# Router logits of a fused recurrence, linear and mixture-of-experts kernel: from eight float32 matmuls between the transposes to sixteen split-operand matmuls behind the first gate product

## The chip, the core and the metric

The kernel runs on one core of one Trainium2 chip. A core has TensorE (matmuls; in the profile PE, and PEld for the loads of its stationary operand), VectorE (DVE), ScalarE (ACT), GpSimd (POOL) and SyncE (SP), which here only issues transfers. Each engine goes through its own list of instructions in order, and they meet through semaphores. The metric is the device time of one execution in microseconds; lower is better.

## What is computed

The input x has 4 batches of 1024 tokens with 1024 channels. Two layers follow each other, and both first run a bidirectional recurrence over the sequence (exponential decay per channel), whose result multiplies the layer's input. The part that matters here stands behind the second recurrence. Cut to it, the reference says:

```
x = x + ffn0(cond(x, side))              # a 1024x1024 linear layer
c = cond1(x, side)                       # the second recurrence, gated
flat = rmsnorm(c, norm_w)                # z below
logits = flat @ router_w.T               # 32 experts
topk_w, topk_ids = top_k(softmax(logits), 4)
routed = sum over the 4 experts of topk_w * (silu(flat@w1_gate) * (flat@w1_up)) @ w2
shared = silu(flat @ sg) * (flat @ su) @ sd
out = x + routed + shared
```

All of it is float32. The large products are done on operands that were split in two parts in the type fp32r (a high part and the rest), as three matmuls: high by high, high by low, low by high. The router logits are a product of z (1024 channels) with 32 columns.

## The kernel before

Channels lie on the 128 partitions in `CB` = 8 blocks, and the 4096 tokens are worked through in `HALVES` = 8 halves of `HALF` = 512 tokens (`HT` = 4 tiles of 128). The program has three stages. In the first (to about 310 us) the recurrence runs alone, block by block ("units"), on DVE, ACT and POOL. In the second (to about 1990 us) TensorE computes the linear layer and the shared experts half by half, while the units for later batches run between on DVE and ACT. In the third the routed experts run, tile by tile.

A half of the second stage has `STEPS` = 32 steps. Each step is one output block of 128 channels: `product` (L1457) issues 24 matmuls of 128x512. In the steps 0 to 15 of a half these are the 8 blocks of the linear layer (`step_l`) and the 8 blocks of the shared down product of the half before (`step_d`); the steps from 16 on are the gate and up blocks (`step_g`), which need z of the whole half. The work of the other engines hangs on the same step numbers: `fill(h, i, ...)` in each engine's program does what belongs to step i, and is called between the instructions of a unit (`FILLS_PER_UNIT` = 8 calls each). The order is thus written out by hand; there is no scheduler. The first half and the last two stand apart, the halves 1 to 5 are a loop on TensorE.

At step 15 to 16 the norm's root is taken and z is made. On TensorE `square_sums` (L1467) adds up the squares, and behind the product of step 15 stand `out_by_token` (L1493) for the half before and then `by_token(h, o)` for o = 0 to 7: four 128x128 transposes of the block z(o) (L1477) and then one float32 matmul (L1479) that adds this block's share to the logits: stationary operand `rw` with 32 columns, moving operand z(o) with 512. On DVE `root(h)` (L1253 to L1261) is followed by `normalize(h, o)` (L1270), which writes z(o) into one of two buffers `Z[o % 2]`, and by `split_z_lo(h, o - 1)` (L1234), the low part of the block before. Between o = 1 and o = 2 stand the last block of the down product (L1248, not in the first half) and the last residual (L1306). On ACT `zhi` (L800) is the high part, and `rows_copy` (L772) brings the transposed block from PSUM to SBUF. Because z(o) takes the buffer of z(o - 2), `normalize` waits for the logits matmul of o - 2, which is the last that reads it:

```
if o < 2:
    wait(ve, "l_tr", h)
else:
    ve.wait_ge(s["z_lo"], h * CB + (o - 1))
    ve.wait_ge(s["logits"], h * CB + (o - 1))
```

Then ACT copies the logits out of PSUM (L806), TensorE turns them after the product of step 16 (`logits_by_token`, L1486), and DVE adds them to the table `acc` at step 18 (L1314). The routing reads `acc` in the halves 6 and 7.

Of the kernel before, what the change touches and what calls it, by code (L numbers as in the profile page):

```python
# [90 lines left out]
def adaln_moe(nc, x_t, side_t, cond, w_all, u_all, lin_sb, norm_w, router_t, shared_w, expert_w, out):  # L91
# [12 lines left out]
    with ctx:  # L104
# [69 lines left out]
        open_part, past, edge, cap, low, neg_low = (sb(name, 2 * BLOCKS) for name in ("open_part", "past", "edge", "cap", "low", "neg_low"))  # L174
# [4 lines left out]
        rw = sb("rw", CB * EXPERTS)  # L179
# [10 lines left out]
        ramp = sb("ramp", EXPERTS, i32)  # L190
        lsb_neg = sb("lsb_neg", CB)
# [12 lines left out]
        for name in (  # L204
            "k_in x_in ramp consts_in cond_in kc ek ekv euk h_fwd h_edge h_bwd h_all den g_ln g_inv nf n_edge nb "
            "wv_done num num_w newton1 newton2 sig_steps sig_x gated gated_raw ratio ratio_out gated_out "
            "split_hi split_lo split_pe chunk product read_out c_hi c_lo sig1_steps sig1 c1 z sq z_hi z_lo res "
            "z_tr logits sums z_copy z_out mean r_ln r_exp newton_r r_set l_copy l_tr l_acc silu_steps silu_sig "
            "a_hi_s a_lo_s o_tr o_copy o_out prep prep_act masks rt rt_act rt_mask rt_pe cnt_copy "
            "fill_set fill_out add_idx_set apart entry_ready listed_in slots_in cols_set w1_hi w1_lo w2_hi w2_lo w1_read w2_read "  # L210
            "rows_in row_idx_set x_tr x_hi x_lo silu_done act_done a_tr a_hi a_lo y_hi y_lo y_out zero_set "
            "zero_out"
        ).split():
            s[name] = sem(name)
# [162 lines left out]
        def _(sp):  # L377
# [8 lines left out]
            for dst, src in ((uu, u_all), (lsb, lin_sb), (nrm, norm_w), (rw, router_t)):  # L386
                sp.dma_start(dst[:, :], src).then_inc(s["consts_in"], 16)
# [145 lines left out]
        def _(pool):  # L533
# [15 lines left out]
            pool.iota(ramp[:, :], pattern=[[1, EXPERTS]], base=0, channel_multiplier=0).then_inc(s["ramp"], 1)  # L549

# [51 lines left out]
            pool.dma_start(out[TOK:TOK + P, :], SPARE).then_inc(s["y_out"], 16)  # L602
            pool.wait_ge(s["rt_mask"], 1)
# [36 lines left out]
        def _(sc):  # L640
# [134 lines left out]
            def fill(h, i, first, prev, next_):  # L775
                if prev and i == 0:
                    act_hi(h - 1, CB - 1)
                if not before_all(h):
# [81 lines left out]
            sc.activation(lsb_neg[:, :], lsb[:, CB:2 * CB], ACT.Copy, scale=-1.0).then_inc(s["prep_act"], 1)  # L860
# [3 lines left out]
            sc.activation(past[:, :], open_part[:, :], ACT.Ln).then_inc(s["prep_act"], 1)  # L864
            sc.wait_ge(s["prep"], PREP + 9)
# [56 lines left out]
        def _(ve):  # L922
# [15 lines left out]
            ve.tensor_scalar(open_part[:, :], decay[:, :], -1.0, 1.0, ALU.mult, ALU.add).then_inc(s["prep"], 1)  # L938
            ve.wait_ge(s["prep"], PREP + 1)
            ve.scalar_tensor_tensor(open_part[:, :], decay[:, :], 1.0, open_part[:, :], ALU.add, ALU.mult).then_inc(s["prep"], 1)  # L940
            ve.wait_ge(s["prep"], PREP + 2)
            ve.tensor_scalar(open_part[:, :], open_part[:, :], 1e-12, None, ALU.max).then_inc(s["prep"], 1)
            ve.wait_ge(s["prep"], PREP + 3)
            ve.reciprocal(low[:, :], open_part[:, :]).then_inc(s["prep"], 1)
# [6 lines left out]
            ve.tensor_tensor(uu[:, :], uu[:, :], past[:, :], ALU.subtract).then_inc(s["prep"], 1)  # L951
            ve.wait_ge(s["prep"], PREP + 8)
            ve.tensor_scalar(neg_low[:, :], low[:, :], -1.0, None, ALU.mult).then_inc(s["prep"], 1)
            ve.wait_ge(s["prep"], PREP + 9)
# [89 lines left out]
            def rank_start():  # L1044
                ve.wait_ge(s["ratio_out"], 16 * BLOCKS + 1)
                ve.wait_ge(s["ramp"], 1)
                done(ve.tensor_copy(rampf, ramp[:, :]))
# [226 lines left out]
            def fill(h, i, first, prev, next_):  # L1274
# [7 lines left out]
                if not before_all(h):  # L1282
# [128 lines left out]
        def _(pe):  # L1411
            pe.wait_ge(s["masks"], 9)
# [56 lines left out]
            def by_token(h, o):  # L1469
# [3 lines left out]
                if o == 0:  # L1473
                    wait(pe, "l_acc", h)
                    wait(pe, "l_copy", h)
# [53 lines left out]
            def half(h, first):  # L1529
                ks = dict(products(h, first))  # L1530
                for i in range(STEPS):
# [15 lines left out]
                    if i == 2 * CB:  # L1547
                        logits_by_token(h)
# [138 lines left out]
```

## Time and profile before

| | |
|---|---|
| median of 3 runs | 4678.69 us (4672.37, 4686.97, 4678.69) |
| span of the profiled execution | 4682.9 us |
| PE, PEld busy | 4475.7 us (96%), 3545.7 us (76%) |
| DVE, ACT, POOL busy | 2567.2 us (55%), 1789.8 us (38%), 722.8 us (15%) |
| TensorE's granted clock, mean | 0.979 |
| PE in the chain of work that ended last | 80% |

Which of the three times belongs to the profiled execution is not listed; its span lies between the second and the third. A matmul's record is longer than its turn on TensorE, since matmuls are pipelined: turns are read from the distance of starts.
### The profile page before, as it was taken

How to read it: one execution, taken by the hardware profiler on the slowest of the kernel's cores; microseconds unless marked ns; L12 is line 12 of the kernel's file. 1: busy time of each engine (PE TensorE's matmuls, PEld its weight loads, DVE VectorE, ACT ScalarE, POOL GpSimd, SP SyncE). 2: the span in 40 equal slices, each digit the busy share in tenths (PEclk: the TensorE clock that was granted, in tenths of full speed). 3: DMA queues.
4: the chain of work that ended last, by engine and by line, in shares of the span. 5: the costliest groups of instructions: out<-in, count | busy, mean ns of one | idle time of the engine just before them, and what ended most of it. 6: DMA issues, size and time to landing. Idle time of an engine off the chain costs nothing.

```text
span 4682.9 us, 60901 instructions
## 1 busy us (share of the span) xinstructions
PE 4475.7 (96%) x19862; PEld 3545.7 (76%) x19863; DVE 2567.2 (55%) x2765; ACT 1789.8 (38%) x2596; POOL 722.8 (15%) x934
## 2 busy tenths in 40 slices
PE   6777999999999999999999999999999999999998
PEld 2245877777777877878888888888888888888887
DVE  8999999999999653433233434444341253333432
ACT  5665555555555333232222323334231142222321
POOL 1000000000000017211111112112111121111111
PEclk8888999999999999999999999999999999999999
DMA  6675767767676766754344545555552254444543
GB/s 226 235 263 184 274 241 268 251 223 282 240 268 226 270 212 190 251 182 111 95 131 112 170 112 160 171 166 150 182 168 57 61 186 145 112 112 116 161 109 61
DMA packets 247928, 835.08 MB, mean 178 GB/s; under 512 B 28160, under 2 KB 61056, under 8 KB 222976
## 3 DMA queue, kind: packets, MB, share of 16 engines
q1 hardware_dynamic: 172944, 572.77, 34.5%
q0 software_dynamic: 47728, 160.07, 15.5%
q10 hardware_dynamic: 27136, 100.67, 5.8%
q8 instruction: 72, 1.18, 0.1%
q14 instruction: 48, 0.39, 0.0%
HBM read 652.40 MB, written 181.01 MB: 178 GB/s over the span
## 4 chain that ended last, share of the span: by engine, by line
PE 80%; DVE 10%; issue 4%; ACT 3%; DMA 2%; POOL 0%; ACTq 0%; DVEq 0%; POOLq 0%; SPq 0%
PE ps L1593 34%; PE ps L1457 22%; PE ps L1607 16%; PE ps L1526 3%; PE ps L1479 1%; PE ps L1582 1%; DVE work L969 1%; DVE work L975 1%; DMA work<-rows_dram,row_idx 1%; PE ps L1477 1%; PE ps L1467 1%; DVE work L996 1%; DVE work L998 1%; DVE work L972 1%; DVE work L1002 1%
## 5 line engine op out<-in xcount | busy, mean ns | idle before, releaser
L1593 PE MATMUL ps<-halves 128*128 128x512 f32 x7152 | 1698.6, 393 | 3.5 <-DVE halves L1356 2.8
L1593 PEld LDWEIGHTS ps<-halves 128*128 128x128 f32 x7152 | 1338.5, 189 | 279.9 <-DVE halves L1356 3.1
L1457 PE MATMUL ps<-halves 128*128 128x512 f32 x6144 | 1450.2, 395 | 13.7 <-issue 12.5
L1457 PEld LDWEIGHTS ps<-halves 128*128 128x128 f32 x6144 | 1154.1, 189 | 287.2 <-issue 47.8
L1607 PE MATMUL ps<-halves 128*128 128x512 f32 x3576 | 834.9, 389 | 1.3 <-DVE halves L1372 1.3
L1607 PEld LDWEIGHTS ps<-halves 128*128 128x128 f32 x3576 | 671.1, 188 | 140.9 <-DVE halves L1372 1.6
L1356 DVE TENSOR_TENSOR halves<-ps,halves 128x1024 fp32r<-128x1024 f32 x150 | 183.7, 1225 | 905.2 <-ACT halves L852 905.2
L1351 DVE TENSOR_TENSOR halves<-work,halves 128x1024 fp32r<-128x1024 f32 (+1 forms) x320 | 440.2, 1433 | 83.6 <-ACT halves L856 83.3
L852 ACT ACTIVATE halves<-ps 128x1024 fp32r<-128x1024 f32 x150 | 154.0, 1027 | 862.4 <-PE ps L1593 862.4
L576 POOL DMA_INDIRECT out<-work,add_idx x149 | 249.8, 1677 | 1417.3 <-DVE work L1378 1382.2
L856 ACT ACTIVATE halves<-work 128x1024 fp32r<-128x1024 f32 (+1 forms) x320 | 369.1, 1229 | 67.0 <-PE ps L1607 56.5
L1372 DVE TENSOR_TENSOR halves<-ps,halves 128x256 fp32r<-128x256 f32 x298 | 112.4, 419 | 491.7 <-ACT halves L884 491.7
L595 POOL TENSOR_SCALAR work<-work 128x1024 f32<-128x1024 f32 x33 | 106.5, 3226 | 1419.9 <-DMA work<-side_t 1419.9
L884 ACT ACTIVATE halves<-ps 128x256 fp32r<-128x256 f32 x298 | 98.5, 382 | 544.4 <-PE ps L1582 544.4
L1378 DVE TENSOR_SCALAR work<-ps,acc 128x512 f32<-128x512 f32 x149 | 111.6, 749 | 276.4 <-PE ps L1607 266.5
L890 ACT ACTIVATE work<-ps,acc 128x512 f32<-128x512 f32 x149 | 102.1, 685 | 408.5 <-PE ps L1607 388.5
L566 POOL DMA_INDIRECT work<-rows_dram,row_idx x151 | 152.5, 1010 | 123.4 <-POOL row_idx L562 69.0
L1526 PE MATMUL ps<-ident,work 128*128 128x128 f32 x1200 | 157.6, 275 | 12.4 <-DMA work<-rows_dram,row_idx 12.4
L975 DVE TENSOR_TENSOR_SCAN work<-decay,edge_in,work 128x1024 f32<-128x1024 f32 x64 | 154.2, 2409 | 14.2 <-ACT edge_in L680 14.2
L1435 PE MATMUL ps<-plain,ident 128*128 128x512 f32 x128 | 83.0, 736 | 73.6 <-ACT halves L735 73.6
L983 DVE TENSOR_TENSOR_SCAN work<-decay,edge_in,work 128x1024 f32<-128x1024 f32 x64 | 150.7, 2355 | 0.0
L1526 PEld LDWEIGHTS ps<-ident,work 128*128 128x128 f32 x1200 | 137.1, 142 | 13.4 <-DMA work<-rows_dram,row_idx 13.3
(186 smaller groups left out, 3674.4 us busy)
## 6 DMA issues: line engine op xcount, KB each, us to landing
halves<-split_dram SPq DMA_DIRECT2D x512, 512.0 KB, 5.6
work<-expert_w SPq DMA_DIRECT2D x192, 1024.0 KB, 5.5
split_dram<-halves ACTq DMA_DIRECT2D x32, 1024.0 KB, 4.9
plain<-shared_w SPq DMA_DIRECT2D x32, 512.0 KB, 3.2
gated_dram<-work ACTq DMA_DIRECT2D x32, 512.0 KB, 4.1
work<-side_t ACTq DMA_DIRECT2D x32, 512.0 KB, 5.6
work<-x_t ACTq DMA_DIRECT2D x32, 512.0 KB, 3.7
ratio_dram<-work ACTq DMA_DIRECT2D x32, 512.0 KB, 4.2
```

The lines of the kernel that those rows point to most:

```text
L566: pool.indirect_dma_start(hx, None, rows_dram[:, :], bass.IndirectOffsetOnAxis(row_idx[:, :].bitcast(u32), 0)).then_inc(s["rows_in"], 16)
L576: pool.indirect_dma_start(out[:, :], bass.IndirectOffsetOnAxis(add_idx[:, :].bitcast(u32), 0), y, None, compute_op=ALU.add).then_inc(s["y_ ...
L852: sc.activation(xhi, ps_xt[:, :], ACT.Copy).then_inc(s["x_hi"], 1)
L856: sc.activation(whi[q][:, part], staged(q, part), ACT.Copy).then_inc(s["w1_hi" if q < 4 else "w2_hi"], 1)
L975: ve.tensor_tensor_scan(F[:, ::-1], d, F[:, ::-1], edge_in[:, 0:1], ALU.mult, ALU.add).then_inc(s["h_bwd"], 1)
L983: ve.tensor_tensor_scan(G[:, ::-1], d, G[:, ::-1], edge_in[:, 1:2], ALU.mult, ALU.add).then_inc(s["nb"], 1)
L1351: ve.tensor_tensor(wlo[q][:, part], staged(q, part), whi[q][:, part].bitcast(f32), ALU.subtract)\
L1356: ve.tensor_tensor(xlo, ps_xt[:, :], xhi.bitcast(f32), ALU.subtract).then_inc(s["x_lo"], 1)
L1457: last = pe.matmul(bank(k % 4), w, op[:, part], start=(c == 0 and w is w_hi and op is hi), stop=(c == CB - 1 and w is w_lo))
L1526: last = pe.transpose(ps_xt[:, c * P:(c + 1) * P], hx[:, c * P:(c + 1) * P], ident[:, :])
L1593: last = pe.matmul(ps_h[:, a * 512:a * 512 + 512], xp[:, xk * P:(xk + 1) * P], wp[:, rhs], start=(xk == 0 and xp is xhi and wp is whi[q]), ...
L1607: last = pe.matmul(ps_y[:, h * 512:h * 512 + 512], ap_[:, (q * 2 + k) * P:(q * 2 + k + 1) * P], wp[:, rhs:rhs + 512], start=(q == 0 and k ...
```

## The change

The logits matmuls leave `by_token`. The router's weights are split like the other operands: `router` holds for each block the high parts of 32 columns and, side by side with them, their low parts (64 columns, and the stationary operand takes 128, so it holds the next block's 64 as well, whose results nobody reads). A new function `logits(h)` stands behind the product of step 16: for each of the 8 blocks one matmul on the high part of z and one on the low part, 16 fp32r matmuls of 128x512 that add into one bank. `logits_by_token` moves behind the product of step 17, ACT's copy of the logits moves from the end of its step 16 to its step 17, behind the first `silu`, and takes 64 rows; DVE adds the two results by one copy and one addition. `normalize` now waits for the transposes of o - 2. To make room, some small buffers share memory, `iota` of `ramp` moves behind POOL's last unit, and the weights are split once at the start by one ACT and one DVE instruction.

```
-        rw = sb("rw", CB * EXPERTS)
+        router = sb("router", (CB + 1) * 2 * EXPERTS, f32r)
+        router_part = lambda part: router[:, 0:CB * 2 * EXPERTS].rearrange("p (o w e) -> p w o e", w=2, e=EXPERTS)[:, part]
...
-            pool.iota(ramp[:, :], pattern=[[1, EXPERTS]], base=0, channel_multiplier=0).then_inc(s["ramp"], 1)
-
+            pool.memset(router[:, CB * 2 * EXPERTS:].bitcast(f32), 0.0).then_inc(s["masks"], 1)
...
             pool.dma_start(out[TOK:TOK + P, :], SPARE).then_inc(s["y_out"], 16)
+            pool.iota(ramp, pattern=[[1, EXPERTS]], base=0, channel_multiplier=0).then_inc(s["ramp"], 1)
...
                         rows_copy(h, CB - 1)
-                        sc.wait_ge(s["logits"], (h + 1) * CB)
-                        sc.wait_ge(s["z_lo"], h * CB + (CB - 1))
-                        sc.activation(Z0[0:EXPERTS, :], LOGIT_BANK[0:EXPERTS, :], ACT.Copy).then_inc(s["l_copy"], 1)
                     for j in range(CB):
                         if i == step_g(j) + 1:
                             silu(h, j)
+                    if i == 2 * CB + 1:
+                        sc.wait_ge(s["logits"], h + 1)
+                        sc.activation(Z0[0:2 * EXPERTS, :], LOGIT_BANK[0:2 * EXPERTS, :], ACT.Copy).then_inc(s["l_copy"], 1)
...
-            sc.activation(lsb_neg[:, :], lsb[:, CB:2 * CB], ACT.Copy, scale=-1.0).then_inc(s["prep_act"], 1)
+            sc.activation(router_part(0), rw.rearrange("p (o e) -> p o e", e=EXPERTS), ACT.Copy).then_inc(s["prep_act"], 1)
...
+            ve.tensor_tensor(router_part(1), rw.rearrange("p (o e) -> p o e", e=EXPERTS), router_part(0).bitcast(f32), ALU.subtract)\
+                .then_inc(s["prep"], 1)
...
                     ve.wait_ge(s["z_lo"], h * CB + (o - 1))
-                    ve.wait_ge(s["logits"], h * CB + (o - 1))
+                    ve.wait_ge(s["z_tr"], h * CB + (o - 1))
...
-                        ve.tensor_copy(acc[:, ds(h * (HT * EXPERTS), HT * EXPERTS)].rearrange("p (t e) -> p t e", t=HT),
-                                       Z_BANK.rearrange("p (t e) -> p t e", t=HT)[:, :, 0:EXPERTS]).then_inc(s["l_acc"], 1)
+                        at = acc[:, ds(h * (HT * EXPERTS), HT * EXPERTS)].rearrange("p (t e) -> p t e", t=HT)
+                        by_part = Z_BANK.rearrange("p (t e) -> p t e", t=HT)
+                        ve.tensor_copy(at, by_part[:, :, 0:EXPERTS]).then_inc(s["l_high"], 1)
+                        ve.wait_ge(s["l_high"], h + 1)
+                        ve.tensor_tensor(at, by_part[:, :, EXPERTS:2 * EXPERTS], at, ALU.add).then_inc(s["l_acc"], 1)
...
-                pe.matmul(LOGIT_BANK[0:EXPERTS, :], rw[:, o * EXPERTS:(o + 1) * EXPERTS], Z[o % 2], start=(o == 0), stop=(o == CB - 1))\
-                    .then_inc(s["logits"], 1)
+
+            def logits(h):
+
+                wait(pe, "l_copy", h)
+                pe.wait_ge(s["z_lo"], (h + 1) * CB)
+                for o in range(CB):
+                    both = router[:, o * 2 * EXPERTS:o * 2 * EXPERTS + P]
+                    for op in (zhi, zlo):
+                        last = pe.matmul(LOGIT_BANK, both, op[:, o * HALF:(o + 1) * HALF], start=(o == 0 and op is zhi),
+                                         stop=(o == CB - 1 and op is zlo))
+                last.then_inc(s["logits"], 1)
...
                     if i == 2 * CB:
+                        logits(h)
+                    if i == 2 * CB + 1:
                         logits_by_token(h)
```

TensorE's list around step 16 of the first half, before (the last three of the eight pairs, the product of step 16, the turning of the logits, the products from step 17 on):

```order
51 L1477 MATMUL ps<-ident,work 128x128 x4
52 L1479 MATMUL ps<-work,rw 32x512
53 L1477 MATMUL ps<-ident,work 128x128 x4
54 L1479 MATMUL ps<-work,rw 32x512
55 L1477 MATMUL ps<-ident,work 128x128 x4
56 L1479 MATMUL ps<-work,rw 32x512
57 L1457 MATMUL ps<-halves 128x512 x24
58 L1486 MATMUL ps<-ident,work 128x128 x4
59 L1457 MATMUL ps<-halves 128x512 x360
```

The same place in the changed kernel, where the lines are nine further on (L1466 is `product`, L1485 the transposes, L1495 the new `logits`):

```order
40 L1476 MATMUL ps<-work,ones 128x512 x3
41 L1485 MATMUL ps<-ident,work 128x128 x32
42 L1466 MATMUL ps<-halves 128x512 x24
43 L1495 MATMUL ps<-halves,router 128x512 x16
44 L1466 MATMUL ps<-halves 128x512 x24
45 L1503 MATMUL ps<-ident,work 128x128 x4
46 L1466 MATMUL ps<-halves 128x512 x336
```

The 32 transposes stand alone in front of step 16's product, and 16 matmuls and the whole of step 17 now stand between that product and the turning of the logits.

DVE's list at step 18 of the first half, in the middle of a unit, before (L1314 takes the logits, L1218, L1224 and L1229 belong to the first gate and up blocks, the others to the unit):

```order
217-215 L975 SCALAR_TENSOR_TENSOR work<-decay,edge_in,work 128x1024
218-216 L979 SCALAR_TENSOR_TENSOR work<-work,cap 128x1024
219-217 L980 SCALAR_TENSOR_TENSOR work<-work,cap 128x1024
220-218 L983 SCALAR_TENSOR_TENSOR work<-decay,edge_in,work 128x1024
221:219 L1314 COPY acc<-ps 128x128
222-220 L1218 TENSOR_TENSOR work<-ps,work 128x512
223-221 L1224 TENSOR_TENSOR work<-ps,work 128x512
224-222 L988 TENSOR_TENSOR work<-work 128x1024
225-223 L1229 TENSOR_TENSOR halves<-work,halves 128x512
```

and in the changed kernel (L1321 and L1323 take the logits):

```order
221-219 L988 SCALAR_TENSOR_TENSOR work<-decay,edge_in,work 128x1024
222:220 L1321 COPY acc<-ps 128x128
223:221 L1323 TENSOR_TENSOR acc<-ps,acc 128x128
224-222 L1223 TENSOR_TENSOR work<-ps,work 128x512
225-223 L1229 TENSOR_TENSOR work<-ps,work 128x512
226-224 L993 TENSOR_TENSOR work<-work 128x1024
227-225 L1234 TENSOR_TENSOR halves<-work,halves 128x512
```

Nothing changes places here; one addition joins, and what the first of them waits for (the turned logits) comes one product and 16 matmuls later in TensorE's list.

## Rows read from the trace of the kernel before

**Rows 1.** Busy time by engine in two stretches of 100 us.

```profile
core 0: us, PE busy (x) PEld busy (x) DVE busy (x) ACT busy (x) POOL busy (x), PEclk, DMA share, GB/s
300.00:400.00 100.00, 64.29 (x216) 44.42 (x216) 96.03 (x77) 56.98 (x74) 8.72 (x3) 0.80 0.59 210
500.00:600.00 100.00, 98.89 (x431) 78.45 (x430) 97.34 (x84) 57.54 (x79) 7.43 (x2) 1.00 0.79 287
```

**Rows 2.** What TensorE waited for between 418 and 1862 us (total, times, longest).

```profile
PE ps L1477 <- DVE work L1270: 19.7, 8, 3.2
PE ps L1457 <- issue: 12.5, 5, 3.1
PE ps L1467 <- ACT work L785: 2.4, 7, 0.3
PE ps L1493 <- ACT work L768: 1.8, 5, 0.6
```

**Rows 3.** The eight stretches from a half's first transpose to step 16's product, PE alone.

```profile
403.90:418.44 14.54, 14.54 (x49) 0.85 0.00 0
608.41:622.44 14.03, 14.03 (x48) 0.88 0.11 37
1024.33:1037.15 12.82, 12.57 (x48) 1.00 0.12 39
1231.72:1247.01 15.29, 15.29 (x49) 0.80 0.09 30
sum 113.85, PE 113.60; mean PE 14.20
```

**Rows 4.** TensorE in time order, at 1.2 and at 2.4 GHz.

```profile
403.90 1.11 PE L1477 MATMUL ps<-ident,work 128*128 128x128 f32 x4 [11.89 <-DVE work L1270]
404.94 1.92 PE L1479 MATMUL ps<-work,rw 128*32 128x512 f32 x2
406.79 1.12 PE L1477 MATMUL ps<-ident,work 128*128 128x128 f32 x4
...
1029.34 0.66 PE L1477 MATMUL ps<-ident,work 128*128 128x128 f32 x4
1029.92 1.05 PE L1479 MATMUL ps<-work,rw 128*32 128x512 f32 x2
1030.90 0.66 PE L1477 MATMUL ps<-ident,work 128*128 128x128 f32 x4
```

**Rows 5.** DVE in time order, in the stretch that begins at 1024.33.

```profile
1026.97 0.75 DVE L1270 SCALAR_TENSOR_TENSOR work<-plain,nrm,work 128x512 f32<-128x512 f32 x1
1027.63 0.69 DVE L1234 TENSOR_TENSOR halves<-work,halves 128x512 fp32r<-128x512 f32 x1
1028.35 0.75 DVE L1270 SCALAR_TENSOR_TENSOR work<-plain,nrm,work 128x512 f32<-128x512 f32 x1
...
1029.74 0.75 DVE L1270 SCALAR_TENSOR_TENSOR work<-plain,nrm,work 128x512 f32<-128x512 f32 x1
```

**Rows 6.** Stretches in which TensorE only runs products, PE alone.

```profile
338.80:343.40 4.60, 4.60 (x11) 0.50 1.00 333
1080.00:1100.00 20.00, 20.00 (x90) 1.00 0.47 160
```

**Rows 7.** DVE in time order: step 14, the next unit's start, step 18.

```profile
1015.02 0.69 DVE L1248 TENSOR_TENSOR work<-ps,work 128x512 f32<-128x512 f32 x1 [1.06 <-PE ps L1457]
...
1036.26 1.22 DVE L963 TENSOR_TENSOR work<-work 128x1024 f32<-128x1024 f32 x1
...
1048.87 0.27 DVE L1314 COPY acc<-ps 128x128 f32<-128x128 f32 x1
...
1054.62 0.69 DVE L1229 TENSOR_TENSOR halves<-work,halves 128x512 fp32r<-128x512 f32 x1 [3.03 <-ACT halves L763]
```

**Rows 8.** All engines between two by-token stretches, with the clock.

```profile
1037.00:1231.00 194.00, 188.17 (x821) 151.74 (x820) 182.50 (x156) 106.02 (x147) 12.73 (x4) 0.99 0.76 267
```

**Rows 9.** The start, in time order: DVE's last preparation, and what opens the first unit.

```profile
14.35 0.20 DVE L953 TENSOR_SCALAR neg_low<-low 128x64 f32<-128x64 f32 x1
15.97 1.06 ACT L660 ACTIVATE work<-work 128x1024 f32<-128x1024 f32 x1 [3.39 <-POOL work L595]
```

More of the change, by code:

```diff
@@ L173, in adaln_moe @@
         uu = sb("uu", 2 * BLOCKS)
-        open_part, past, edge, cap, low, neg_low = (sb(name, 2 * BLOCKS) for name in ("open_part", "past", "edge", "cap", "low", "neg_low"))
+        edge, cap, low, neg_low = (sb(name, 2 * BLOCKS) for name in ("edge", "cap", "low", "neg_low"))
+        open_part, past, rw = N[:, 0:2 * BLOCKS], N[:, 2 * BLOCKS:4 * BLOCKS], N[:, 4 * BLOCKS:4 * BLOCKS + CB * EXPERTS]
         edge_in = sb("edge_in", 2)
@@ L189, in adaln_moe @@
         add_idx = sb("add_idx", 1, i32)
-        ramp = sb("ramp", EXPERTS, i32)
-        lsb_neg = sb("lsb_neg", CB)
+        ramp = uu[:, 0:EXPERTS].bitcast(i32)
+        lsb_neg = ww[:, 0:CB]
         eps = sb("eps", 1)
@@ L207, in adaln_moe @@
             "split_hi split_lo split_pe chunk product read_out c_hi c_lo sig1_steps sig1 c1 z sq z_hi z_lo res "
-            "z_tr logits sums z_copy z_out mean r_ln r_exp newton_r r_set l_copy l_tr l_acc silu_steps silu_sig "
+            "z_tr logits sums z_copy z_out mean r_ln r_exp newton_r r_set l_copy l_tr l_high l_acc silu_steps silu_sig "
             "a_hi_s a_lo_s o_tr o_copy o_out prep prep_act masks rt rt_act rt_mask rt_pe cnt_copy "
@@ L385, in _ @@
             sp.dma_start(work[:, 0:BATCH * COND], cond.to_broadcast([P, BATCH * COND])).then_inc(s["cond_in"], 16)
-            for dst, src in ((uu, u_all), (lsb, lin_sb), (nrm, norm_w), (rw, router_t)):
-                sp.dma_start(dst[:, :], src).then_inc(s["consts_in"], 16)
+            for dst, src in ((uu[:, :], u_all), (lsb[:, :], lin_sb), (nrm[:, :], norm_w), (rw, router_t)):
+                sp.dma_start(dst, src).then_inc(s["consts_in"], 16)
             def load_piece(h, k, step):
@@ L863, in _ @@
             sc.wait_ge(s["prep"], PREP + 3)
-            sc.activation(past[:, :], open_part[:, :], ACT.Ln).then_inc(s["prep_act"], 1)
-            sc.wait_ge(s["prep"], PREP + 9)
+            sc.activation(past, open_part, ACT.Ln).then_inc(s["prep_act"], 1)
+            sc.activation(lsb_neg, lsb[:, CB:2 * CB], ACT.Copy, scale=-1.0).then_inc(s["prep_act"], 1)
+            sc.wait_ge(s["prep"], PREP + 10)
             side_exp(0)
@@ L937, in _ @@
             ve.wait_ge(s["consts_in"], 64)
-            ve.tensor_scalar(open_part[:, :], decay[:, :], -1.0, 1.0, ALU.mult, ALU.add).then_inc(s["prep"], 1)
+            ve.tensor_scalar(open_part, decay[:, :], -1.0, 1.0, ALU.mult, ALU.add).then_inc(s["prep"], 1)
             ve.wait_ge(s["prep"], PREP + 1)
-            ve.scalar_tensor_tensor(open_part[:, :], decay[:, :], 1.0, open_part[:, :], ALU.add, ALU.mult).then_inc(s["prep"], 1)
+            ve.scalar_tensor_tensor(open_part, decay[:, :], 1.0, open_part, ALU.add, ALU.mult).then_inc(s["prep"], 1)
             ve.wait_ge(s["prep"], PREP + 2)
-            ve.tensor_scalar(open_part[:, :], open_part[:, :], 1e-12, None, ALU.max).then_inc(s["prep"], 1)
+            ve.tensor_scalar(open_part, open_part, 1e-12, None, ALU.max).then_inc(s["prep"], 1)
             ve.wait_ge(s["prep"], PREP + 3)
-            ve.reciprocal(low[:, :], open_part[:, :]).then_inc(s["prep"], 1)
+            ve.reciprocal(low[:, :], open_part).then_inc(s["prep"], 1)
             ve.wait_ge(s["prep"], PREP + 4)
@@ L1046, in rank_start @@
                 ve.wait_ge(s["ramp"], 1)
-                done(ve.tensor_copy(rampf, ramp[:, :]))
+                done(ve.tensor_copy(rampf, ramp))
                 done(ve.tensor_scalar(rev, rampf, -1.0, float(EXPERTS), ALU.mult, ALU.add))
@@ L1411, in _ @@
         def _(pe):
-            pe.wait_ge(s["masks"], 9)
+            pe.wait_ge(s["masks"], 10)
+            pe.wait_ge(s["prep"], PREP + 10)
             pe.wait_ge(s["consts_in"], 64)
@@ L1474, in by_token @@
                     wait(pe, "l_acc", h)
-                    wait(pe, "l_copy", h)
                 for t in range(HT):
```

4 lines of the change are left out of this document (2 added, 2 removed).

## Prediction

> **What bounds the kernel now.** I read the page first, then busy time by stretches, the waits, the order of time and the granted clock around step 16 of each half.
>
> In the second stage TensorE is the bound. Between the first half's transposes and the last half's it waits for little: some 2.5 us per half for the first z, some 3 us at each turn of the loop on its own instruction stream, and next to nothing else [rows 2]. DVE is close behind, 97.34 of 100 us busy in one such stretch [rows 1] and 182.50 of 194 us in another [rows 8]. Step 14's product holds it 1.06 us before one half ends [rows 7], so TensorE still sets that date. An edit on TensorE's list thus moves the end about one for one, as long as DVE doesn't fall behind it.
>
> The place of the change is the stretch from a half's first transpose to step 16's product. It lasts 12.82 to 15.29 us, 113.85 us over the eight halves, and PE is never idle in it [rows 3]. It is paced by TensorE's pairs: at 2.4 GHz four transposes take 0.58 us and a float32 logits matmul 0.98 us (starts 1029.34, 1029.92, 1030.90), together 1.56 us; at 1.2 GHz 1.04 and 1.85 us [rows 4]. The length differs by clock: 12.82 us where it was granted 1.00, 15.29 us at a mean of 0.80 [rows 3]. The low spells begin with TensorE's wait for the root and end while transposes and matmuls follow each other without a gap.
>
> **The change, step by step.**
>
> *Removed: the eight matmuls in the stretch.* They take 8 x 0.98 = 7.8 us a half, but the stretch doesn't shrink by that. Without them it goes at DVE's pace: z(o) and the low part of the block before. Where DVE didn't wait, z followed z at 1026.97 and 1028.35, then 1029.74: 1.39 us [rows 5]. Four transposes need 0.58 or 1.04 us and fit in that at either clock. z(2) begins 2.64 us after the first transpose (1026.97 less 1024.33), z(7) five times 1.39 us later at 9.6, ends at 10.35, and its transposes bring step 16's product to 11.4 us at 1.2 GHz, 10.95 at 2.4. The first half has no L1248 (0.7 us) and comes to 10.7. Sum at the low clock: 7 x 11.4 + 10.7 = 90.5 us against 113.85, so **-23.3 us**; at the high clock 7 x 10.95 + 10.3 = 87.0, so -26.9.
>
> *Added: sixteen matmuls behind step 16's product.* They have the form of the products': 90 in 20.00 us, 0.222 us each [rows 6]. 16 x 0.222 = 3.55 us a half, **+28.4 us** in all. Nothing on TensorE hides them, since it has no wait behind that place but those of rows 2, and these are tied to later dates.
>
> By the count of passes alone it would be 7.8 removed and 3.55 added, -34 us. The Trainium skill (FP8 and Floating Point Precision, Matmul Precision, the notes on TensorE's precision) says that true float32 takes four passes through the array. By that rule a float32 logits matmul is worth four turns and its two replacements two, so TensorE does less than before; the rule speaks of TensorE's work and not of the pace that DVE sets here.
>
> *The clock at step 16's product.* Before, the stretch is TensorE work without a gap, and step 16's product always found 2.4 GHz. After, TensorE works 0.58 us of each 1.39 us at the high clock and 1.04 of 1.39 at the low one, for 10 us, behind a wait of 2.5 us. A near case is the first stage: PE 64% busy, with gaps, and a mean clock of 0.80 [rows 1]. I expect that the clock is low when step 16's product begins, in nearly all eight halves. In the product at 338.80 the low clock went on for 4.60 us with 11 matmuls in them, 0.418 us each instead of 0.222 [rows 6]: a microsecond at the low clock costs 0.47 us. The spells before lasted, by the mean clocks of rows 3, 0 us (1.00), 3.4 (0.88), 4.4 (0.85) and 6.1 (0.80). A spell that reaches into the product will partly have passed, so I take 3.6 us, the lower middle: 1.7 us a half, **+13.6 us**. Bounds: nothing (clock back before the product), and 6.1 us in the product, 2.9 us a half, +23.
>
> The Trainium skill (TensorE: Matmul & The Clock Gate, Part 4 on the PE-mode transpose) says that a transpose does not count as busy for the clock the way a matmul does. No row here has transposes alone, so this case can't show it yet. If it holds, step 16's product starts at 1.2 GHz in every half.
>
> *DVE and ACT.* The addition is one more 128x128 pass, about 0.27 us like the copy (L1314) [rows 7], 2 us in eight halves. More important, the turned logits come later: step 16's product at 11.4, its end at 18.4 (24 x 0.222 and 1.7), the logits matmuls to 22.0, step 17's product to 27.3, the turning to 27.9 us after the first transpose. DVE arrived at L1314 at 24.5 (1048.87 less 1024.33) and will now idle some 3.4 us there, in a half in which it has little slack. It gets them back: before L1229 it waited 3.03 us for ACT [rows 7], whose own work there hangs on the step's stores and moves with TensorE. So I cost it at nothing. If that cover were gone, DVE would be 3.4 + 0.3 us later and TensorE itself -2.9 + 3.55 + 1.7 = 2.3, so 1.4 us a half, in the six halves with units +9. ACT's copy stands behind the first `silu`, which waits for step 16's product anyway and ends about when the logits are done. In the last two halves DVE idles much more, so routing isn't touched.
>
> *Start and the rest.* One ACT and one DVE instruction more, about 0.4 us. DVE's preparation ended at 14.55, and the first unit waited for POOL until 15.97 [rows 9]: hidden, and 0.4 us if it weren't. `ramp` behind POOL's last unit makes DVE wait a microsecond or two once, in half 6, where it has slack. Zero.
>
> Sum: -23.3 + 28.4 + 13.6 = **+18.7 us**. Against the profiled execution's span, 4682.9 us, that is 4701.6. The median of the runs shown is 4.2 us under this span, so I forecast 4678.7 + 18.7 = **4697 us**, 0.4% slower.
>
> **Rivals.**
>
> 1. *The clock is back in time.* The transposes keep or bring 2.4 GHz. For it: the low clock always ended within the old stretch, and at 1.2 GHz the new one has TensorE working three quarters of the time. Against it: the gaps, and the first stage. Then -26.9 + 28.4 = +1.5 us, 4680: not slower. It decides from the point where fewer than six of the eight products start low (six cost 6 x 1.7 = 10 us, which with the 1.5 to 5.1 of the first two terms comes to the 14 us that a measurement can tell). Chance 0.15.
>
> 2. *DVE sets the pace, and TensorE's extra hides.* For it: DVE is busy 94% of the time between two stretches [rows 8]. Against it: it waited for step 14's product [rows 7], and TensorE waits only for the root. Then the gain is DVE's: it went on with the unit 0.9 us before a stretch's end (L963 at 1036.26 [rows 7], 1037.15 [rows 3]), on average at 14.2 - 0.9 = 13.3 us, and would now at 11.7 (z(7) ends at 10.35, then ACT's high part and its own low part, some 0.65 us each). 1.6 us earlier, less 0.3 for the addition: 8 x -1.3 = -10 us, 4668. It decides if the wait for the root shrinks by what TensorE does more. Chance 0.13.
>
> 3. *DVE falls behind at the later logits.* The 3.4 us at L1314 aren't covered by the 3.03 us at L1229, and the next root comes later than TensorE asks. +18.7 + 9 = +28 us, 4706. For it: the little slack of rows 8. Chance 0.07.
>
> 4. The forecast, a low clock at most products: 0.65. Its own range begins at +9 us (the first two terms give 5.1, and 8 x 0.5 us if the clock is back one microsecond into each product) and ends at +28 (5.1 and the upper bound of 23): 4688 to 4707.
>
> **How the numbers follow.** About 0.3%, 14 us, is what a measurement can tell from no change. Of the forecast's case some three quarters lie above +14 us and the rest within; rival 3 lies above; rival 1 is within; rival 2 lies mostly within, with a tail beyond -14. Slower: 0.65 x 0.75 + 0.07 = 0.55. Faster: 0.07. Same: 0.38. The range takes in the forecast's, rival 3 and rival 1, and leaves out rival 2 and the tails: 4676 to 4711.
>
> **What the changed profile would show.** The stretch from first transpose to step 16's product about 11 us in each half, with z 1.39 us apart and PE idle between groups of four transposes; 16 matmuls of the new line about 0.22 us apart; a granted clock of 0.50 at the start of step 16's product and 10 to 12 matmuls of it at 0.42 us; DVE idle for the turned logits at step 18 and no longer for ACT right behind them; the wait for the root as before, 2.3 to 3.2 us. I am wrong if the clock reads 1.00 at these starts (rival 1), if the root's wait is gone (rival 2), or if it has grown (rival 3).

## The result, and the profile of the changed kernel

| | before | changed |
|---|---|---|
| median of 7 runs each, us | 4678.69 (4672.37 to 4686.97) | 4697.42 (4688.68 to 4702.05) |
| span of the profiled execution, us | 4682.9 | 4694.0 |
| its mean granted clock | 0.979 | 0.973 |

The ratio is 1.0039, with a 95% interval of 1.0030 to 1.0048: slower by 0.4%. The forecast was 4697 us, with a range of 4676 to 4711. The changed kernel was measured again beside the later experiments: 4694.74 against 4680.84 us, ratio 1.0032 (1.0020 to 1.0044). Its distance from the kernel before is thus 11.1 us by the two spans, 13.9 and 18.7 us by the two pairs of medians.

The page of the changed kernel, its first two parts in excerpt:

```profile
span 4694.0 us, 60897 instructions
## 1 busy us (share of the span) xinstructions
PE 4459.2 (95%) x19860; PEld 3579.8 (76%) x19863; DVE 2570.2 (55%) x2774; ACT 1789.4 (38%) x2597; POOL 723.9 (15%) x935
```

Shares of 40 slices don't show what happened. As before the change, one has to go to the ten microseconds in front of step 16's product. This is the sum of the changed kernel's waits on TensorE in the second stage (total, times, longest), to be held against [rows 2]:

```profile
PE ps L1485 <- DVE work L1275: 41.9, 49, 3.6
PE ps L1466 <- issue: 11.6, 5, 2.9
PE ps L1510 <- ACT work L770: 2.6, 5, 1.4
PE ps L1476 <- ACT work L787: 2.4, 7, 0.3
```

The wait of the transposes for z (now L1485 and L1275) came 8 times and comes 49 times, seven in each of seven halves: TensorE now waits at nearly every block. The 3 us stalls on its own stream are as they were, 11.6 against 12.5 us.

The eight stretches from a half's first transpose to step 16's product, TensorE alone, for the changed kernel (length, busy time, granted clock):

```profile
404.39:414.82 10.43, 8.31 (x33) 0.50 0.00 0
608.97:620.12 11.15, 7.66 (x33) 0.57 0.17 57
...
1030.65:1041.80 11.15, 8.31 (x33) 0.50 0.16 53
...
sum 88.48, PE 63.88; mean PE 7.98
```

Against [rows 3] two things changed. From the second half on the length no longer varies, 11.15 us at a clock of 0.50 as at 0.57, because DVE sets it; and the clock, which was 0.80 to 1.00, is 0.50 to 0.62. What follows is step 16's product, again TensorE alone, from its first matmul to the first logits matmul; its eight lengths are between these:

```profile
414.82:420.93 6.11, 6.11 (x27) 0.91 0.21 68
...
831.39:839.02 7.63, 7.63 (x27) 0.71 0.19 60
1041.80:1048.39 6.59, 6.59 (x26) 0.83 0.23 70
...
sum 54.37, PE 54.37; mean PE 6.80
```

In the kernel before, the same 24 matmuls always took 5.60 us. Two of its eight:

```profile
622.44:628.04 5.60, 5.60 (x25) 1.00 0.25 84
1037.15:1042.75 5.60, 5.60 (x26) 1.00 0.28 84
```

The half that begins at 1030.65 in order of time on TensorE, with the idle time before a group and what ended it in brackets:

```profile
1030.65 1.97 PE L1485 MATMUL ps<-ident,work 128*128 128x128 f32 x8 [2.29 <-DVE work L1275]
1034.09 1.11 PE L1485 MATMUL ps<-ident,work 128*128 128x128 f32 x4 [1.47 <-DVE work L1275]
1035.47 1.12 PE L1485 MATMUL ps<-ident,work 128*128 128x128 f32 x4 [0.28 <-DVE work L1275]
...
1041.80 6.76 PE L1466 MATMUL ps<-halves 128*128 128x512 f32 x24
1048.39 3.83 PE L1495 MATMUL ps<-halves,router 128*128 128x512 f32 x16
1052.06 5.62 PE L1466 MATMUL ps<-halves 128*128 128x512 f32 x24
```

Groups of four transposes start 1.39 us apart, last 1.11 us at the low clock, and wait 0.28 us for the next z. Then come the product at a rising clock and the sixteen logits matmuls (L1495), 3.67 us from start to start, 0.229 us each. DVE in the same half, where it takes the turned logits:

```profile
1058.59 0.29 DVE L1321 COPY acc<-ps 128x128 f32<-128x128 f32 x1 [3.62 <-PE ps L1503]
1058.91 0.29 DVE L1323 TENSOR_TENSOR acc<-ps,acc 128x128 f32<-128x128 f32 x1
...
1063.86 0.69 DVE L1234 TENSOR_TENSOR halves<-work,halves 128x512 fp32r<-128x512 f32 x1 [2.19 <-ACT halves L765]
```

DVE now waits 3.62 us for the turning, where it waited for nothing [rows 7], and its wait for ACT behind it fell from 3.03 to 2.19 us. Two sums of DVE's waits in the second stage (total, times, longest): in the kernel before, from 608 to 1862 us, `normalize` waited for the logits matmuls of the stretch, which it no longer does:

```profile
DVE work L1270 <- PE ps L1479: 12.4, 33, 1.5
```

In the changed kernel, from 608 to 1881 us, it waits for the turned logits instead:

```profile
DVE acc L1321 <- PE ps L1503: 35.6, 6, 16.2
```

### The profile page after: what moved, and what is told of

The parts are those of the page before. It is cut to its first block, busy times and chain, and to the rows that moved or that the text cites. A ratio compares the mean times of both kernels' runs of the same rounds, so it can differ in the third digit from the quotient of the medians.

```text
span 4694.0 us, 60897 instructions
## 1 busy us (share of the span) xinstructions
PE 4459.2 (95%) x19860; PEld 3579.8 (76%) x19863; DVE 2570.2 (55%) x2774; ACT 1789.4 (38%) x2597; POOL 723.9 (15%) x935
## 4 chain that ended last, share of the span: by engine, by line
PE 78%; DVE 11%; issue 5%; ACT 3%; DMA 2%; POOL 0%; DVEq 0%; POOLq 0%; ACTq 0%; SPq 0%
PE ps L1612 33%; PE ps L1466 22%; PE ps L1626 16%; PE ps L1543 3%; PE ps L1601 1%; DVE work L974 1%; DVE work L980 1%; DMA work<-rows_dram,row_idx 1%; DVE work L1001 1%; PE ps L1476 1%; DVE work L1003 1%; DVE work L1275 1%; DVE work L977 1%; PE ps L1495 1%; DVE work L1007 1%
## 5 line engine op out<-in xcount | busy, mean ns | idle before, releaser
L1466 PE MATMUL ps<-halves 128*128 128x512 f32 x6144 | 1458.9, 397 | 12.6 <-issue 11.6
L1466 PEld LDWEIGHTS ps<-halves 128*128 128x128 f32 x6144 | 1162.5, 190 | 281.8 <-issue 39.9
L1543 PE MATMUL ps<-ident,work 128*128 128x128 f32 x1200 | 157.5, 275 | 12.4 <-DMA work<-rows_dram,row_idx 12.4
```

Of the source, the lines that this page charges most:

```text
L1466: last = pe.matmul(bank(k % 4), w, op[:, part], start=(c == 0 and w is w_hi and op is hi), stop=(c == CB - 1 and w is w_lo))
L1543: last = pe.transpose(ps_xt[:, c * P:(c + 1) * P], hx[:, c * P:(c + 1) * P], ident[:, :])
```

## The experiments

My theory after this: TensorE sets the end, so the three terms (a shorter stretch, sixteen matmuls in the open, that is behind the stretch and in nobody's wait, and a low clock in step 16's product) add up one for one. Its rivals: DVE sets the date, and TensorE's extra work is hidden; or the low clock is no consequence of the gaps between transposes. Added matmuls in what follows write to the logits' bank ahead of its real use or again with the same numbers, and leave the output as it is.

Six of the kernels below, in two comparisons on two chips (four and two kernels), all took about 130 us longer, and so did the kernel before beside them (4809.27 and 4813.63 us). In the six the time lies in one place near the end of stage two that the last section tells of; of the kernel before no trace was taken there. Ratios to the kernel before are what counts in these.

**The logits product issued twice** (of the changed kernel). It asks what 3.6 us more of TensorE behind step 16's product cost.

```diff
-                for o in range(CB):
+                for o in [*range(CB), *range(CB)]:
```

> The changed kernel with its sixteen logits matmuls issued twice in a row (the second pass starts the sum again, so the result is the same). Theory A, TensorE's turns behind step 16's product are on the path: 8 x 16 more matmuls at 0.229 us (3.67 us for 16 in the changed kernel's trace) add 29 us, 4697 becomes 4726, 1.0% over the kernel before; DVE's wait at L1321 grows by 3.7 us a half. Rival, DVE or ACT sets the pace in the halves with units and TensorE has slack there: at most the two last halves pay, +7 to +12 us, 4704 to 4709.

Measured: 4873.01 us, ratio 1.0136 (1.0121 to 1.0150), which is 0.97% or some 47 us over the changed kernel's 1.0039. TensorE in order of time, at one logits product and at the next turn of the loop:

```profile
626.87 7.49 PE L1495 MATMUL ps<-halves,router 128*128 128x512 f32 x32
634.19 5.63 PE L1466 MATMUL ps<-halves 128*128 128x512 f32 x24
...
719.86 0.96 PE L1466 MATMUL ps<-halves 128*128 128x512 f32 x3 [2.98 <-issue]
723.84 8.45 PE L1466 MATMUL ps<-halves 128*128 128x512 f32 x26 [3.03 <-issue]
```

The 32 matmuls take 7.33 us from start to start, 3.66 more than 16, so 29 us in eight halves: all of it, and more, is in the time. DVE's wait for the turned logits grew with them, by 3.7 us a half as expected. Nothing hides TensorE's work here, and the rival of a DVE that sets the date falls. The other 18 us were in neither expectation. TensorE's stall on its own stream at the turn of the loop, as a rule one a turn in the changed kernel, now came twice at each: 24.4 us in 8 stalls up to 1700 us, 12.8 us more, and each pair with a spell of low clock.

**Ten matmuls into the wait for the root** (of the changed kernel), where TensorE idles 2.3 to 3.6 us. Does the clock stay up in the stretch if it is up when the stretch begins?

```diff
+            def keep_busy(n):
+                for _ in range(n):
+                    pe.matmul(LOGIT_BANK, ahi_s[:, 0:P], ahi_s[:, 0:HALF], start=True, stop=True)
...
                     if i == 2 * CB - 1:
+                        keep_busy(10)
                         for o in range(CB):
                             by_token(h, o)
```

> The changed kernel with ten useless matmuls (their bank is overwritten later) in TensorE's wait for the root, 2.2 us at 2.4 GHz, so that it enters the transposes from steady work. Theory A1, the transposes alone don't hold the clock: it falls somewhere in the stretch, step 16's product still starts at 1.2 GHz in most halves and takes 6.2 to 7.6 us instead of 5.3; time 4697, within 5 us. Rival, it is the idle wait before the transposes that brings the low clock into the product: the product starts at 1.00, and 10 to 12 us come back, 4686.

Measured: 4832.79 us, ratio 1.0051 (1.0039 to 1.0063), some 6 us over the changed kernel's 1.0039, where 5 at most were expected; the intervals overlap. The stalls at the loop's turns came to 20.5 us in 8, against 11.6 in 5. TensorE in order of time, transposes now at L1490:

```profile
604.76 1.32 PE L1490 MATMUL ps<-ident,work 128*128 128x128 f32 x8
608.20 0.66 PE L1490 MATMUL ps<-ident,work 128*128 128x128 f32 x4 [2.12 <-DVE work L1275]
609.59 1.12 PE L1490 MATMUL ps<-ident,work 128*128 128x128 f32 x4 [0.73 <-DVE work L1275]
...
615.91 7.29 PE L1466 MATMUL ps<-halves 128*128 128x512 f32 x24
```

The stretch begins at 2.4 GHz (8 transposes in 1.32 us, 4 in 0.66), and from the group at 609.59 on it is at 1.2 (4 in 1.12 us), behind nothing but transposes and the wait of 2.12 us among them. Seven of the eight stretches begin high and end low like this. The product is as slow as in the changed kernel, 55.42 us over the eight against 54.37. So the low clock at step 16 isn't left over from the wait: it is made inside the stretch.

**The same, and two matmuls behind each block's transposes.** `keep_busy(2)` is added behind `last.then_inc(s["z_tr"], 1)`.

> The same with two more useless matmuls behind each block's four transposes, in the gap that DVE's pace of 1.39 us leaves (0.58 + 0.44 us at 2.4 GHz). Theory A: the clock stays at 1.00 from the root's wait on, step 16's product takes 5.3 us in all eight halves, the stretch stays at about 11 us, and the low clock's share comes back: 11.7 us by the changed kernel's trace (54.4 us for eight products less 42.7), 4685 to 4686. Rival, the low clock costs nothing since something else waits anyway: 4697 as before. If the gap is smaller than I take it, the stretch grows and the gain is less.

Measured: 4812.47 us, ratio 1.0008 (1.0000 to 1.0017), 0.31% below the changed kernel's 1.0039 and 0.24% below its second ratio: 12 to 15 us back. The stretch and the product behind it, TensorE alone:

```profile
603.30:614.65 11.35, 8.60 (x50) 1.00 0.17 53
614.65:620.10 5.45, 5.45 (x26) 1.00 0.25 83
```

The clock is 1.00 throughout here, the stretch is still 11.35 us (DVE's pace again), and the product is at 5.45. All eight products ran at 1.00, 43.70 us in all and 10.7 less than in the changed kernel; the stretches took 1.6 us more. Useless work made the kernel faster, by about what the low clock took. The Trainium skill (TensorE: Matmul & The Clock Gate, Part 4) says that a transpose doesn't count as busy for the clock the way a matmul does. These two runs agree with it: with transposes alone the granted clock fell to 0.50 even from 1.00, and with two matmuls behind each four transposes it was 1.00. They don't prove it, since the matmuls added work as well as changed its kind, and no run added as much work in transposes.

**The real pairs in place of the useless ones.** If matmuls between the transposes are wanted, the logits' own are there. The pair of each block is issued one block later, behind its low half.

```diff
                 last.then_inc(s["z_tr"], 1)
+                if o:
+                    logits(h, o - 1)
...
-                        logits(h)
+                        logits(h, CB - 1)
```

`logits(h, o)` waits for `z_lo` of its block and issues its two matmuls; the wait for the bank (`l_copy`) moves to block 0.

> The changed kernel with the two logits matmuls of block o - 1 behind the transposes of block o, so that only the last pair stands behind step 16's product. Theory A: 14 of 16 matmuls go into the gaps of DVE's pace and the work in them ends the low clock before the product. At 2.4 GHz the stretch is 11.4 us, plus about 1 us where it begins at 1.2 GHz, plus 0.45 us for the last pair: 12.9 us a half against 14.2 before, so -11 us against the kernel before, 4668, and 29 under the changed kernel. Rival, the gap doesn't hold them (the low part of block o - 1 comes too late, or the pace grows): the stretch is 14 us or more and the time that of the kernel before, 4679.

Measured: 4797.73 us, ratio 0.9980 (0.9971 to 0.9989), the first that is faster than the kernel before, and by about what was expected. The stretch is 11.56 us (10.84 in the first half) and the product runs at 1.00 in all eight halves. One wait is new, in order of time on TensorE behind step 17's product:

```profile
1040.82 0.60 PE L1512 MATMUL ps<-ident,work 128*128 128x128 f32 x4
1042.72 0.66 PE L1505 MATMUL ps<-ident,work 128*128 128x128 f32 x4 [1.30 <-ACT work L811]
```

ACT's copy of the logits (L811) is late for the turning at step 17, 7.7 us in six halves.

**The pairs, with the turning one step later.** Turning at step `2 * CB + 2`, DVE's copy and addition at `2 * CB + 3`.

```diff
-                    if i == 2 * CB + 1:
+                    if i == 2 * CB + 2:
                         logits_by_token(h)
```

> The pairs in the stretch, and the logits turned one product later (behind step 18, DVE takes them at step 19). With the pairs alone TensorE waited 1.28 us a half for ACT's copy of the logits, which stands behind the first silu. Theory: that wait goes and nothing takes its place, 8 x 1.28 = 10 us less than the 11.5 us that the pairs gained: ratio 0.9955. Rival, DVE or ACT is late there anyway, so the time is that of the pairs alone, ratio 0.998.

Measured beside the changed kernel's second measurement: 4664.68 us (4662.61 to 4667.96), ratio 0.9970 (0.9958 to 0.9982). It beats both kernels, by 16 us the one before and by 30 us the changed one. The wait for ACT's copy is gone from TensorE's waits, but the gain over the pairs alone is smaller than expected (0.9970 and not 0.9955), and the intervals of the two overlap. TensorE in order of time in one half:

```profile
1015.05 1.78 PE L1486 MATMUL ps<-ident,work 128*128 128x128 f32 x8 [2.95 <-DVE work L1275]
1016.48 1.20 PE L1496 MATMUL ps<-halves,router 128*128 128x512 f32 x2
1018.50 1.11 PE L1486 MATMUL ps<-ident,work 128*128 128x128 f32 x4 [0.81 <-DVE work L1275]
...
1023.01 0.60 PE L1486 MATMUL ps<-ident,work 128*128 128x128 f32 x4
...
1026.04 0.74 PE L1496 MATMUL ps<-halves,router 128*128 128x512 f32 x2
1026.62 5.61 PE L1466 MATMUL ps<-halves 128*128 128x512 f32 x24
1032.07 0.62 PE L1496 MATMUL ps<-halves,router 128*128 128x512 f32 x2
```

The stretch starts at the low clock and is at the high one before the product; all eight products take 43.71 us, at 1.00. Of the sixteen matmuls fourteen lie almost wholly in time that DVE's pace leaves open, and the last pair (0.46 us) is in the way. Two effects come together here, and the rows part them. The place: the stretches take 91.73 us, 3.3 more than in the changed kernel, and 3.7 us of logits are in the open instead of 29.4, together -22.4 us. The clock: -10.7 us in the products, as in the run with the useless matmuls. The sum is -33 us, and 30 were measured.

**The pairs turned late, and ten matmuls in the wait.** If the clock were up from the start, would the stretch shrink more?

> The same with the ten useless matmuls in the wait for the root. The pairs alone left step 16's product at 2.4 GHz in all but one half, and the stretch at 11.6 us where 11.35 was reached at a steady 2.4 GHz; so at most 0.2 us a half, 2 us, ratio within 0.0005 of the kernel without them. Rival, that the clock still costs something in the stretch: 5 us or more.

Measured: 4674.05 us, ratio 0.9989 (0.9980 to 0.9998), 9 us above the kernel without the filler, where 2 at most were expected to change. The stretch stayed at 11.56 us, so the clock early in it is worth nothing, DVE being the pace. The loss is elsewhere: stalls of TensorE on its own stream came 7 times, up to 3.7 us, with 17.3 us in all up to 1700 us, against 11.6 in 6 without the filler. And in 100 us around the four turns of the loop (25 us each) the mean granted clock was 0.90 instead of 0.97.

**The filler in the kernel before.** There the stretch was TensorE's own, and 12.82 us at a clock of 1.00 [rows 3], so the same ten matmuls should save time.

> The kernel before with ten useless matmuls in TensorE's wait for the root (2.2 us at 2.4 GHz). Theory A: the low clock that its stretches had (14.2 us on average against 12.8 us in the one at a granted clock of 1.00) is gone, so each half but the first, whose wait of 11.9 us they don't fill, has a stretch of 12.8 us: 7 x 1.4 = 10 us less, ratio 0.998. Rival, the low clock comes from the transposes themselves and not from the wait: stretches as before, ratio 1.000.

Measured: 4682.71 us, ratio 1.0001 (0.9992 to 1.0010). One of its stretches, and TensorE's waits on its own stream up to 1700 us:

```profile
603.79:616.61 12.82, 12.57 (x50) 1.00 0.13 40
```

```profile
PE ps L1457 <- issue: 16.8, 7, 2.9
```

The stretches did shrink, to 103.55 us in all, 10.3 less, and seven of eight were at 1.00. The expected 10 us didn't come out in the time. They were lost within the loop: from the second half's first transpose to the seventh's it took 1037.6 us (603.79 to 1641.41), the kernel before 1036.0 (608.41 to 1644.37), though the five stretches in between had lost 7 us. TensorE stalled twice at three of the four turns, 16.8 us in all against 12.5, and around the turns the mean clock was 0.93 instead of 0.97. That this accounts for all of the loss is not shown.

**The same filler with 32 columns** (of the kernel before), to have as many instructions and hardly any work. I took it that so little work wouldn't raise the clock, and that the stalls would come all the same.

```diff
-                    pe.matmul(LOGIT_BANK, ahi_s[:, 0:P], ahi_s[:, 0:HALF], start=True, stop=True)
+                    pe.matmul(LOGIT_BANK[:, 0:32], ahi_s[:, 0:P], ahi_s[:, 0:32], start=True, stop=True)
```

> The kernel before with the ten useless matmuls in the wait for the root cut to 32 columns each: ten instructions more in the loop of the halves 1 to 5, next to no work. Theory: what took the gain of the ten long ones back is the number of instructions, since TensorE's own stream stalls twice instead of once at the loop's turns (7 waits of 16.8 us in all there, against 5 of 12.5 before, each followed by a low clock). Then the stretches are as before, 13 to 15 us with low spells, and each turn of the loop costs 1.5 to 2 us more: 6 to 8 us slower, ratio 1.0015. Rival, the long matmuls themselves got in the way of the root or of the clock: ratio 1.000, with the waits at the turns as before.

Measured: 4821.52 us, ratio 1.0020 (1.0011 to 1.0029), near the expected 1.0015, but not for the reason given. The stalls came, 17.3 us in 7. On the clock I was wrong. One of its stretches:

```profile
607.39:620.22 12.83, 12.57 (x49) 1.00 0.15 49
```

Five of seven were 12.8 us at a clock of 1.00. So the stretches gained here too, 7 us over the five in the loop, and the loop still took 3.4 us longer than in the kernel before: some 11 us were lost in it, and the stalls grew by 4.8 only. The clock around them has a part in the rest. 25 us around the loop's second turn, in this kernel and in the kernel before:

```profile
918.00:943.00 25.00, 20.59 (x72) 0.80 0.74 257
```

```profile
917.00:942.00 25.00, 20.82 (x85) 0.93 0.79 273
```

Over the four turns (100 us) the mean clock is 0.86, against 0.97, so some 20 us more were at the low level. At 0.47 us for a microsecond at the low clock that is an estimated 10 us at most, since TensorE also stands still in part of that time.

**Filler only outside the loop** (of the pairs turned late). If the stalls follow the number of instructions in the loop's body, they should be as without filler when the ten matmuls stand only in the halves written out ahead of it and behind it.

```diff
+                        if isinstance(h, int):
+                            keep_busy(10)
```

> The pairs in the stretch, turned late, with the ten long matmuls only in the three halves that stand outside the loop. Theory: the loop has its old length, so its turns are as without them (waits of some 11.6 us), the 9 us that the fill cost in all halves are back, and the clock in the three halves is worth nothing more: ratio 0.997. Rival, the fill costs what it did because of its work: 0.998 or more.

Measured: 4808.04 us, ratio 0.9990 (0.9981 to 0.9999), and not the expected 0.997. TensorE's waits on its own stream up to 1700 us:

```profile
PE ps L1466 <- issue: 20.3, 8, 3.2
```

The loop's body is the one that gave 0.9970, where the stalls were 11.6 us in 6, and it now stalls twice at each turn; from the second half's first transpose to the seventh's it took 1036.8 us instead of 1023.3. The theory that the number of instructions in the body decides falls. What remains is that the stalls depend on where the body lies behind the code ahead of it. That is argued and not shown: no run here moved the body alone, and this kernel was measured on another chip than the one without filler.

## Why the prediction was right

**The bound.** TensorE sets the end of stage two: right. Its work behind step 16's product came out in the time in full when it was doubled. Two readings of the old stretch were a little too neat. PE idles 0.25 us in the stretch at 1024.33 ([rows 3] has 12.57 of 12.82 busy), and two of its low spells begin just behind its first transpose and not in the wait. Neither enters the sum.

**The stretch, -23.3 us.** 88.48 us against 113.85 [rows 3], so -25.4 us. DVE's pace of 1.39 us was right to the hundredth. The 2.1 us come from the last block: its transposes hold the product up by 0.77 us (1041.03 to 1041.80), not by the 1.04 us that they take.

**The logits in the open, +28.4 us.** 8 x 3.67 = +29.4 us: 0.229 us each and not 0.222. The 90 matmuls that I divided 20.00 us by [rows 6] include some that only reach over the window's ends; 88 begin in it, 0.227 us apart.

**The clock, +13.6 us.** The mechanism was right, and the price too high. The product began at the low clock in all eight halves, and took 54.37 us instead of 8 x 5.60 = 44.8: +9.6 us, 1.2 us a half and not 1.7. The term that I mis-sized is the 3.6 us of low clock in the product. At 0.47 us a microsecond, 1.2 us is 2.6 us of it, and the granted clock of the eight products gives 2.6 us as well, from 1.1 to 4.4. I had taken that length from spells in the old stretch, where TensorE worked without a gap.

**The sum** of what was measured is -25.4 + 29.4 + 9.6 = +13.6 us. The date at which TensorE leaves the last half's logits (1880.57) lies 13.0 us behind the one at which it left step 16's product before (1861.96 + 5.60 = 1867.56). That agrees with the second pair of medians, 13.9 us; the spans give 11.1 and the first pair 18.7 us. That the first pair meets the forecast's +18.7 us to the decimal is luck: its terms are some 5 us too high together, within what separates two measurements.

**DVE.** It idles 3.62 us at the turned logits where I wrote 3.4, 3.3 to 4.7 us in the five halves of the loop. It is covered, since the wait for the root remained (2.26 to 3.58 us a half, 19.4 us in seven halves; before 2.3 to 3.2 and 19.5), but only in part by what I named. The wait for ACT behind it isn't gone, as I wrote that it would be: in these five halves it fell by 0.8 to 1.5 us. A second part I didn't see: DVE's 33 waits for the logits matmuls inside the stretch, 12.4 us, are gone. So the term of nothing was right, and its reason half right. The remaining wait for the root refutes rival 2, whose sign was that wait gone, and rival 3, whose sign was that wait grown by 1.4 us a half. Rival 1 is refuted by the clock at eight of eight products. The run with matmuls in the wait and in the stretch shows what it would have been: 1.0008, close to that rival's +1.5 us.

**The start and the rest.** The first transpose of the first half came 0.49 us later (404.39 for 403.90), where I had written zero or 0.4. It says little: the second trace of the changed kernel has it at 402.37.

**What I didn't see** is that the worse half of the edit was its place. Sixteen matmuls of half the price are the better arithmetic; the loss is that they left a stretch which DVE paces, and in which fourteen of them cost 0.4 us a half instead of 3.2. I wrote both halves of this (the stretch has TensorE idle, the added work is in the open) and costed them, and gave no thought to the pairs in the stretch, which is the faster kernel.

## What to carry to other kernels

When work is moved off an engine's stretch, look at who sets the pace there afterwards: if another engine does, the room that the move makes is idle time, and the new, shorter work would have been almost free in the old place. A stretch of transposes with gaps had a price beyond the gaps here, since the matmuls behind it started at half the clock; a few matmuls between them brought it back, best the useful ones. And before a gain of a few microseconds in a loop is believed, look at the stalls on the engine's own instruction stream at the loop's turn: in several kernels here a second one came there with the edit, and the loop lost what the edit had won, or more.

## What the runs showed of the hardware that I had not expected

TensorE's stream stalls for 2.1 to 3.8 us at each turn of the loop, and at some turns once more, for 0.2 to 4.9 us, a few microseconds later. Up to 1700 us it was 16.8 us in 7 stalls for the kernel before with a filler, 24.4 us in 8 for the doubled logits, 10.8 us in 4 for the kernel with both fillers; a spell of low clock comes with most of them. One kernel varies too: the two traces of the changed kernel have 11.6 us in 5 and 12.6 us in 7, and 1042.9 and 1046.8 us from the second half's first transpose to the seventh's.

Ten matmuls of 32 columns, with their 128-column weight loads, in the wait for the root left the clock at 1.00 over the stretch in five of seven halves (one of seven without them).

In the six kernels of the two slower comparisons TensorE got one matmul each 2 to 3 us for about 130 us in the seventh half, 50 to 54 stalls of 102 to 108 us in all, while POOL issued the indirect DMAs of the routing. The kernel with the pairs in the stretch, TensorE alone around it and then both engines in order of time:

```profile
1600.00:1700.00 100.00, 96.55 (x433) 0.98 0.57 191
1745.00:1875.00 130.00, 28.27 (x50) 0.50 0.09 25
```

```profile
1773.34 0.58 PE L1466 MATMUL ps<-halves 128*128 128x512 f32 x1 [2.22 <-issue]
1773.81 0.97 POOL L587 DMA_INDIRECT slots_dram<-acc  x1 [0.30 <-issue]
1774.75 0.28 PEld L1466 LDWEIGHTS ps<-halves 128*128 128x128 f32 x1 [2.52 <-issue]
...
1776.14 0.58 PE L1466 MATMUL ps<-halves 128*128 128x512 f32 x1 [2.22 <-issue]
```

By the profile TensorE waits for no semaphore there, only for its next instruction. In the other comparisons the same code ran without it, in the kernel before as in the changed one: the kernel before issued its 112 indirect DMAs in that place too, and PE was busy 127 of the 130 us from 1745 to 1875. What brings it on was not tried and stays open.
